# Thirty-six unread transposes on TensorE around the first two norms of a three-stage block kernel

## The reference

```
x = x + 0.5 * ternary_ffn(layernorm(x))
x = x + attention_block(layernorm(x))      # linear attention, 16 heads of 64, then a GELU FFN
x = x + 0.5 * ternary_ffn(layernorm(x))

ternary_ffn(h):                            # weights -1, 0, 1, with a scale for each output
    h = silu(h @ W1 * s1) * (h @ W2 * s2)  # 128 -> 512
    h = gelu(h @ H1 * t1)                  # 512 -> 512
    h = gelu(h @ H2 * t2)                  # 512 -> 512
    return h @ W3 * s3                     # 512 -> 128
```

## Time and profile before

| | us |
|---|---|
| median of 3 runs | 836.9 |
| lowest and highest of them | 836.72, 838.37 |
| the profiled execution | 837.59 |
| its span, first to last instruction | 835.8 |
| TensorE (PE) busy in it | 794.1 (95%) |
| VectorE (DVE), ScalarE (ACT), GpSimd (POOL) busy | 560.4, 566.9, 355.4 |

### The profile page before, as it was taken

One profiled execution on the slowest core, in us unless ns is written; L12 is line 12 of the kernel. 1 busy time (PEld: TensorE's weight loads), 2 busy tenths in 40 slices (PEclk: granted clock), 3 DMA queues, 4 the chain that ended last, 5 costly groups with the idle time before them and its releaser, 6 DMA issues.

```text
span 835.8 us, 27765 instructions
## 1 busy us (share of the span) xinstructions
PE 794.1 (95%) x11682; PEld 672.9 (81%) x11682; DVE 560.4 (67%) x1315; ACT 566.9 (68%) x1019; POOL 355.4 (43%) x283
## 2 busy tenths in 40 slices
PE   2989999999999999999999999999889999999997
PEld 2767888877888888988888988888777888888886
DVE  5967447445867868777886877876979582828220
ACT  3586778768556666566666566666678877778774
POOL 4697979765100101010010101000246697979784
PEclk9999999999999999999999999999999999999999
DMA  7011102021000101010010100201115220201011
GB/s 239 1 51 44 58 20 57 18 72 50 17 3 2 50 0 51 0 38 13 0 51 0 51 0 13 76 0 38 29 53 150 80 63 13 63 12 52 1 51 28
DMA packets 56700, 33.53 MB, mean 40 GB/s; under 512 B 1984, under 2 KB 55232, under 8 KB 56640
## 3 DMA queue, kind: packets, MB, share of 16 engines
q1 hardware_dynamic: 56640, 32.79, 13.6%
HBM read 22.29 MB, written 10.49 MB: 39 GB/s over the span
## 4 chain that ended last, share of the span: by engine, by line
PE 66%; ACT 12%; DVE 10%; issue 4%; POOL 3%; DMA 1%; SPq 0%; DVEq 0%; ACTq 0%; POOLq 0%
PE ps L713 30%; PE ps L892 15%; PE ps L674 7%; PE ps L955 4%; PE ps L966 4%; ACT ee L1284 3%; ACT rr L1285 3%; PE ps L786 3%; PE ps L982 2%; DVE ol L1737 2%; PE ps L938 2%; ACT vt L1306 2%; ACT kf L1314 1%; POOL alB L1855 1%; POOL alA L1855 1%
## 5 line engine op out<-in xcount | busy, mean ns | idle before, releaser
L1284 ACT ACTIVATE ee<-ps 128x512 f32<-128x512 f32 x128 | 78.3, 611 | 92.8 <-PE ps L892 66.3
L1955 POOL TENSOR_TENSOR as<-as,power 128x4 f32<-128x4 f32 x16 | 19.0, 1187 | 282.3 <-DVE as L1660 252.0
L1855 POOL TENSOR_TENSOR alA<-full,ahA 128x512 fp32r<-128x512 f32 x82 | 112.5, 1384 | 38.5 <-DVE ahA L1458 20.7
L1855 POOL TENSOR_TENSOR alB<-full,ahB 128x512 fp32r<-128x512 f32 x84 | 110.6, 1327 | 23.3 <-ACT ahB L1166 7.2
L713 PE MATMUL ps<-ahA,wh 128*128 128x512 f32 x288 | 115.0, 399 | 1.7 <-POOL alA L1855 1.7
L1450 DVE SCALAR_TENSOR_TENSOR full<-ps,sc,gate 128x512 f32<-128x512 f32 x64 | 46.6, 747 | 101.7 <-PE ps L713 60.8
L713 PE MATMUL ps<-ahB,wh 128*128 128x512 f32 x288 | 113.4, 394 | 0.6 <-POOL alB L1855 0.6
L713 PE MATMUL ps<-alA,wh 128*128 128x512 f32 x288 | 113.2, 393 | 0.0
L713 PE MATMUL ps<-alB,wh 128*128 128x512 f32 x288 | 112.3, 390 | 0.0
L1165 ACT ACTIVATE full<-ps,sc 128x512 f32<-128x512 f32 x86 | 59.4, 690 | 40.1 <-PE ps L713 23.0
L1285 ACT ACTIVATE rr<-ps 128x512 f32<-128x512 f32 x128 | 78.8, 616 | 0.0
(11 more groups left out here) (188 smaller groups left out, 2166.4 us busy)
## 6 DMA issues: line engine op xcount, KB each, us to landing
wst<-in_ternary SPq DMA_DIRECT2D x5, 512.0 KB, 8.6
stage<-in_attn SPq DMA_DIRECT2D x4, 512.0 KB, 5.2
xlnA<-x_scratch SPq DMA_DIRECT2D x8, 256.0 KB, 2.8
axr<-x_scratch SPq DMA_DIRECT2D x8, 256.0 KB, 3.1
yx_scratch<-ay SPq DMA_DIRECT2D x8, 256.0 KB, 2.3
xs_scratch<-axs SPq DMA_DIRECT2D x8, 256.0 KB, 2.4
xlnA<-yx_scratch SPq DMA_DIRECT2D x8, 256.0 KB, 2.8
xlnB<-yx_scratch SPq DMA_DIRECT2D x8, 256.0 KB, 2.9
```

Source lines behind the costliest of these rows:

```text
L1284: nc.scalar.activation(ee[k][:, :], src[:, :], ACT.Exp).then_inc(*X["act"].step(f"e_{name}"))
L1855: return nc.gpsimd.tensor_tensor(dst, src, hi.bitcast(F32), ALU.subtract)
```

## The change

A helper `unread(count)` issues so many transposes of the 128x128 identity, all into the same 128 columns of bank 5, which nobody reads before the first product in bank 5 overwrites them. They wait for nothing and signal nothing. Twelve are issued ahead of the norm of A, twelve behind it, and twelve behind the norm of B, ahead of the waits and the small product of the flag.

```diff
+            def unread(count):
+                for _ in range(count):
+                    nc.tensor.transpose(ps[5][:, 0:P], ident[:, :], ident[:, :])
+
             all_before(pe, weights)
+            unread(12)
             for u, U in enumerate(PAIR):
                 tern_norm(u, U, 0)
+                unread(12)
             for eng in ("act", "dve"):
                 pe.wait_ge(*weights[eng].done("sum5" if eng == "act" else "sum4", 0))
```

## The result

| | us |
|---|---|
| before, median of 18 runs | 836.59 (835.32 to 839.32) |
| after, median of 18 runs | 833.57 (830.98 to 837.25) |
| ratio | 0.9962, 95% interval 0.995 to 0.9973 |
| the profiled execution of after | 834.15, span 832.4 |

The change makes the kernel 0.38% faster: 3.2 us by the ratio, 3.0 by the medians. Three more sets of runs gave 0.9953, 0.9963 and 0.9959.

A forecast was written before the change was run, and what follows sets the result against it. The prediction took TensorE, busy 95% of the span, as the bound, with DVE's chain limiting gains early on. Transposes cost nothing and the clock gives 0.5 us: 836.9 - 0.5 = 836.4 us, range 834.8 to 838.2.

The forecast's parts named there:

- What the transposes cost: Before 17.25 us on TensorE: 0.22 us each at the low clock, 0.11 at the high, all hidden, so no cost.
- The second dozen's cover of 0.1 us: Twelve transposes from 9.15 to 11.8 us would end just ahead of the norm of B at 11.89.
- Whether transposes raise the clock: Nearly gapless transposes from 8.27 us should raise TensorE's clock between 11.2 and 12.9 us.
- Rival 2: Transposes on TensorE don't raise the clock; only 36 hidden instructions are added: 836.9 us, chance 0.20.
- Whether the clock falls in the stillness behind the third dozen: TensorE idles 3.0 to 3.5 us before 17.25; clock likeliest down between about 16 and 18.7 us, chance 0.50.
- forecast 0.5: First products: low time at most 3.4 us instead of 4.66, gaining about 0.5 us; chance 0.50.
- rival 1: Clock stays up through the first products from 17.25 us: full 1.9 us gained, 835.0, chance 0.17.
- DVE's cast: Behind DVE's third product: the cast stays stretched to more than 1 us, as POOL's subtraction comes at the same moment.
- DVE's fourth product: With a high clock from 17.25 us it starts at about 22.7 in place of 24.66, 1.9 us earlier.
- at most 3.4 us instead of 4.66: Low-clock time among TensorE's first products after a fall, taken as between 0 and a good 1.2 us less.
- Thirty-six transposes, nothing removed or moved: What the change adds on TensorE before 17.25 us; a dozen takes 2.6 or 1.3 us.
- Bound below: nothing, since no other engine waits for them: Least cost of the added transposes on TensorE: nothing; the bound above had the flag 4.6 us late.

The follow-up runs named there:

- no_third_dozen: The changed kernel without the twelve transposes behind the norm of B, loop not put back in place: 836.12 us, ratio 0.9989 to before.
- place72_again: Repeat of the kernel before with 72 semaphore checks ahead of the attention loop and no unread transposes: 834.77 us, ratio 0.9964 to before.
- place72_only: The kernel before plus 72 semaphore checks ahead of the attention loop, no unread transposes: 834.78 us, ratio 0.9962 to before.
- place256_only: The kernel before plus 256 semaphore checks ahead of the attention loop, no unread transposes: 837.97 us, ratio 1.0008 to before.
- clock_only: The changed kernel plus 184 semaphore checks, so the loop begins 256 instructions later than in before: 835.04 us, ratio 0.9965; repeated, 836.55 us, 0.9984.
- after_third: The changed kernel, unchanged, in a further set of runs: 835.17 us, ratio 0.9963 to before.
- narrow36: The changed kernel with each unread transpose replaced by an unread one-column product of the identity: 842.30 us, ratio 1.0065 to before.
- after_again: The changed kernel, unchanged, as a second profile and set of runs: 832.89 us, ratio 0.9953 to before.
- third24: The changed kernel with 24 transposes in the third dozen's place and 232 semaphore checks ahead of the loop: 833.71 us, ratio 0.9959 to before.
- fill_all_four: The changed kernel plus 160 checks and unread transposes behind the flag and ahead of work at 46, 76 and 585 us: 830.74 us, ratio 0.9919 to before.

## Why the prediction was wrong

- **What the transposes cost: right.** 0.22 us each at the low clock (2.79 us a dozen), half at the high (1.47 us), the flag not late (15.51 against 15.91 us). The second dozen's cover of 0.1 us held.
- **Whether transposes raise the clock: they do.** Rival 2 is out. In no_third_dozen the clock rose at 7.30 us, when TensorE had run nothing but twelve transposes. In the twelve profiles with unread transposes of 128 columns it rose first at 6.82 to 14.19 us, in the five without any at 19.98 to 22.85.
- **Whether the clock falls in the stillness behind the third dozen: half right.** Of six profiles with 36 transposes it fell in three, at 17.06 to 17.84 us, as forecast, and stayed up in three. The falls in the earlier trace rows after 2.6 and 2.1 us of stillness made me take a fall after 3 us for likely. Such a stretch can pass: which of the two it is changes from execution to execution of one kernel.
- **What each course is worth: right.** With a fall the first stage was 0.8 us shorter (forecast 0.5), without one 2.0 (rival 1: 1.9). The chain through DVE up to `xnA` shows it with less scatter. From the first product to the transposes of `xnA` it was 28.98 to 29.01 us in four profiles without transposes (28.41 in place72_again), 27.98, 28.51 and 28.50 with 36 and a fall, 26.75, 27.22 and 26.74 with 36 and none. Two steps of the working were off and did little harm. DVE's cast didn't stay stretched: in after it took 0.43 us at 20.99, though a subtraction of POOL started at that moment too, as one ran beside the 1.28 us of before (from 23.16), so that running beside it doesn't by itself stretch the cast. And DVE's fourth product came 4.75 us behind TensorE's first, against 7.41 in before, a gain of 2.7 us there and not 1.9. And "at most 3.4 us instead of 4.66" means at least 1.2 us less, where I went on with "between 0 and a good 1.2". (4.66 us lie between the first product of before, 17.25 us, and the first rise in its record of the clock, 21.91.) The step's mean is 1.4 and not 0.5, so the term was mis-sized, by its chances (0.50 to 0.17 for an even choice).
- **The step that failed** is "Thirty-six transposes, nothing removed or moved", with its "Bound below: nothing, since no other engine waits for them". It took the transposes for time on TensorE alone. They are also 72 instructions ahead of a loop, and everything behind them in TensorE's program moves. place72_only has the changed kernel's gain without a single transpose, and place256_only has none. That term was missing, about 1.9 us by the stages, and the earlier trace rows hold no row of it, though the view of waits had one: 1.9 us at line 938 with "issue" as the reason. With it and 1.4 us for the clock the sum is 836.9 - 3.3 = 833.6, against 833.57 measured, within the errors given above.

What is shown and what isn't: that the place in the program gives a gain by itself, that 256 instructions bring it back to nothing, and that the cut sits at a fixed instruction (49 products into the group, or 13 when the program is 72 instructions longer) is shown. That TensorE waits there for the next 16 KB of its program is my reading of the times of the packets of q8 and of a count. None starts between 262.0 and 587.8 us in before, while TensorE repeats the loop. Here is the last packet that started ahead of the product behind the cut:

| | packet's end, us | the product starts, us | idle time |
|---|---|---|---|
| before, 50th product | 220.63 | 222.02 | 1.32 |
| clock_only, 50th | 219.22 | 220.67 | 1.56 |
| after_third, 14th | 218.61 | 220.07 | 0.94 |
| place72_again, 14th | 217.59 | 219.02 | 0.92 |
| after, 14th | 214.82 | 218.11 | none |
| place72_only, 14th | 216.41 | 220.45 | none |

In all 18 profiles, each of the 34 idle times of TensorE with the reason "issue" between 200 and 262 us ended 1.2 to 1.6 us behind the end of a packet. With the loop 72 or 328 instructions later the group ran through without a step in seven profiles, and in all of them the packet had ended 3.3 us or more ahead of the 14th product. So the gain of the place is that the packet mostly comes early enough. Why it does so behind the move, and why it came late in after_third and place72_again all the same, isn't shown. The count is of TensorE's instructions in the traces, those counted in that only check semaphores or set registers. In before 256 of them (124 products, 124 weight loads, 8 others) lie between the idle times at 248.02 and 252.40 us, with one packet of q8, and 1280, which is 5 times 256, between those at 222.02 and 248.02, with five packets. Of the 34 idle times just named, 33 have 2497 instructions ahead of them in their profile or a multiple of 256 more; the last, of narrow36, has 3266, one beside such a multiple. That, and place256_only, gives a packet 256 instructions here, 64 bytes for each. In the group of 64 small products, which starts a new one every 0.015 us, TensorE stood still for 1.0 to 1.6 us in each profile with the loop in its old place.

Open: by time, the place alone measured 3.0 to 3.2 us, more than the 1.9 of the stages, and the clock alone 2.9 and then 1.3. By time the parts sum to more than the whole, by stages they don't; the intervals of the ratios are 2 to 3 us wide and don't settle it. A low stretch near 590 us, worth 1.5 us by my estimate, comes in some profiles of one kernel and not in others (589.17 in after, none in after_again), and one near 180 us came only in kernels with transposes and the moved loop; whether the change alters how often they come isn't settled. third24, whose first stage is 1.2 us shorter than the mean with 36, didn't beat the changed kernel by time, which fits a late flag in executions where the clock is low behind the norm of B, but no profile caught one.

## What to carry to other kernels

Filling waits of TensorE with unread transposes cut the time that its clock was low (10.9 us of the first stage without them, 8.5 with 36), but didn't make a fall impossible: it fell among the first products in three of six profiles with 36, and in fill_all_four, where they reached up to the first product. With either the first or the last dozen left out the clock's gain was hardly to be seen (first stage 185.11 to 185.94 us, against a mean of 185.6 without any), and with three more waits filled the kernel was 0.8% faster than before. An edit that adds or takes instructions ahead of a loop with dense small products may also move the points at which TensorE stands still in it, as 72 instructions moved one by 36 products here, which was worth as much as the edit's own effect (1.9 us against 1.4 by the stages); test for it with the same count of idle instructions and no work, and with 256 of them, which here left the point at the same product. Idle time with the reason "issue" in a group of small instructions, here 1.2 to 1.6 us behind the end of a packet of the instruction queue, is the row to look for before predicting.

## What the runs showed of the hardware

- The rise and the fall of the clock aren't fixed to the kernel's own time: with the same instructions it rose at 12.32, 11.01, 6.96 and 11.84 us in four profiles of the changed kernel.
- In narrow36, weight loads and one-column products, with the norms' eight transposes among them and nearly without a gap from 3.8 to 20.9 us, didn't raise the clock. It rose only at 26.2 us, 4.1 us behind the first product of 512 columns.
- Between the first rise of the clock and the low stretch in which each profile ends, the 18 profiles have 48 low stretches. 44 were 3.4 us long (17.84 to 21.25 in after_again, 43.04 to 46.45 in after), four twice that, 6.8 us (14.13 to 20.95 in no_third_dozen).
- The granted clock is on record as 1.00 or 0.50, nothing between. The column reads 1.00 up to the first rise too, where the durations say that it is low: in before up to 21.9 us, with 128x512 products of 0.63 us at 21.22 and 0.39 at 22.48.
- TensorE stood still until 1.2 to 1.6 us behind the end of a 16 KB packet of q8, 34 times in 18 profiles between 200 and 262 us; with the loop 72 or 328 instructions later, the second group of small products ran without a step in the seven profiles in which the packet had ended 3.3 us or more ahead of its 14th product.
- Of these 34 idle times, 33 lie at an instruction with 2497 ahead of it, or a multiple of 256 more.
